# Hybrid two-layer network on one core: the scan's first convolution tap and the retention decays' clip written by ScalarE

## The reference, cut to what matters

```python
# scan: causal depthwise convolution of 4 taps over tokens, 256 channels
xp = jnp.pad(x_proj, ((0, 0), (D_CONV - 1, 0), (0, 0)))
x_conv = conv_b + sum((xp[:, k:k + l, :] * conv_w[:, k] for k in range(D_CONV)))
x_conv = _silu(x_conv)

# retention: per head and per one of 2 mixtures a decay, then a recurrence over tokens
beta = jnp.clip(jax.nn.sigmoid((x @ Wbeta.T + bbeta).reshape(b, t, NH, M)), BMIN, BMAX)   # 0.85, 0.9995
K = K * bt[..., None] + pk[:, :, None, :]
S = S * bt[..., None, None] + pk[:, :, None, :, None] * vt[:, :, None, None, :]
```

## Time and profile before

| | |
|---|---|
| median of 3 runs | 2204.74 us (2204.45 to 2205.43) |
| the profiled execution's own time | 2204.35 us |
| its span | 2202.6 us |
| busy: TensorE, VectorE, ScalarE, GpSimd | 1956.4, 1684.0, 1038.3, 491.6 us |
| mean granted TensorE clock | 0.948 of full |
| scan, first to last instruction | 0 to 206 us |
| retention | 771 to 1050 us |
| steady scan tile, from one first multiply-add of half 0 to the next (104.64 to 126.29) | 21.65 us |
| VectorE's wait for the copy L454 in the scan's tiles 1 and 3 | 1.58, 0.57 us |

### The profile page before, as it was taken

One profiled execution on the slowest core, in us unless ns is written; L12 is line 12 of the kernel. 1 busy time (PEld: TensorE's weight loads), 2 busy tenths in 40 slices (PEclk: granted clock), 3 DMA queues, 4 the chain that ended last, 5 costly groups with the idle time before them and its releaser, 6 DMA issues. The chain is left out here.

```text
span 2202.6 us, 35939 instructions
## 1 busy us (share of the span) xinstructions
PE 1956.4 (89%) x12434; PEld 1468.8 (67%) x12434; DVE 1684.0 (76%) x5253; ACT 1038.3 (47%) x1617; POOL 491.6 (22%) x556
## 2 busy tenths in 40 slices
PE   5786799998999966673899979999999999989999
PEld 3554699987899823332799955556556556559998
DVE  6997788876888879998788877766766666627887
ACT  3442244433444434442444445665655665554443
POOL 1110100012000022320200024543544544330000
PEclk8998999999999987876899989999999999989999
DMA  3000100000000010000000000000000000000000
GB/s 100 6 5 4 56 1 1 1 1 1 1 1 1 1 40 1 0 1 0 1 1 1 1 1 1 1 1 1 1 1 1 1 1 1 1 1 11 11 8 14
DMA packets 17639, 15.75 MB, mean 7 GB/s; under 512 B 4210, under 2 KB 16178, under 8 KB 16947
## 3 DMA queue, kind: packets, MB, share of 16 engines
q1 hardware_dynamic: 15152, 12.66, 1.8%
q10 hardware_dynamic: 2306, 0.78, 0.2%
HBM read 10.55 MB, written 2.88 MB: 6 GB/s over the span
## 5 line engine op out<-in xcount | busy, mean ns | idle before, releaser
L2284 DVE TENSOR_REDUCE soft_mx<-psum 128x1 f32<-128x512 f32 (+3 forms) x608 | 380.7, 659 | 196.8 <-PE psum L2153 109.3
L2199 ACT ACTIVATE soft_prob<-psum 128x1024 f32<-128x1024 f32 (+3 forms) x384 | 305.1, 813 | 205.9 <-PE psum L2079 204.8
L163 POOL TENSOR_TENSOR norm_rstd<-norm_mv,s_const_minus_half 128x4 f32<-128x4 f32 x64 | 65.2, 1019 | 916.5 <-DVE norm_mv L158 909.6
L2149 PE MATMUL psum<-soft_own,soft_stack 128*128 128x512 f32 (+3 forms) x768 | 250.3, 376 | 15.7 <-DVE soft_mx L2284 13.4
L2079 PE MATMUL psum<-soft_stack,soft_own 128*128 128x512 f32 (+3 forms) x768 | 228.4, 380 | 2.9 <-POOL soft_stack L2056 2.2
L2079 PEld LDWEIGHTS psum<-soft_stack,soft_own 128*128 128x128 f32 x768 | 121.3, 189 | 133.4 <-issue 74.5
L2149 PEld LDWEIGHTS psum<-soft_own,soft_stack 128*128 128x128 f32 x768 | 139.2, 192 | 74.3 <-DVE soft_mx L2284 59.7
L1075 DVE SCALAR_TENSOR_TENSOR x<-psum,ffn1b_cw,x 128x128 f32<-128x128 f32 x512 | 144.2, 344 | 31.3 <-PE psum L949 22.6
L2096 PE MATMUL psum<-soft_prob,soft_v_pad 128*32 128x512 f32 (+3 forms) x1536 | 163.6, 498 | 3.5 <-ACT soft_prob L2199 2.1
L1075 DVE SCALAR_TENSOR_TENSOR x<-psum,ffn0b_cw,x 128x128 f32<-128x128 f32 x512 | 144.2, 344 | 27.1 <-PE psum L949 18.4
L1075 DVE SCALAR_TENSOR_TENSOR x<-psum,ffn0a_cw,x 128x128 f32<-128x128 f32 x512 | 144.2, 344 | 27.1 <-PE psum L949 18.4
(11 more groups left out here) (377 smaller groups left out, 4055.4 us busy)
## 6 DMA issues: line engine op xcount, KB each, us to landing
s_ffn_w<-in_ffn_w SPq DMA_DIRECT2D x4, 1024.0 KB, 7.6
out_x<-x SPq DMA_DIRECT2D x8, 256.0 KB, 2.3
x<-in_x SPq DMA_DIRECT2D x4, 384.0 KB, 7.4
mamba_coef_dram<-mamba_out_coef SPq DMA_DIRECT2D x8, 96.0 KB, 1.6
s_ret_w<-in_ret_w SPq DMA_DIRECT2D x1, 640.0 KB, 3.6
x<-in_x SPq DMA_DIRECT2D x4, 128.0 KB, 3.6
s_ret_cos<-in_ret_cos SPq DMA_DIRECT2D x1, 512.0 KB, 6.8
s_ret_sin<-in_ret_sin SPq DMA_DIRECT2D x1, 512.0 KB, 6.9
```

Source lines behind the costliest of these rows:

```text
L163: self.nc.gpsimd.tensor_tensor(self.rstd[:, :], self.mv[:, :, 1], self.const["minus_half"][:, 0:GT], ALU.pow).then_inc(self.rstd_ready, 1)
L2149: ins = pe.matmul(per_head[:, n, :], stack[:, u % HT, i * P:(i + 1) * P], own[:, u % 3, g, half * BLK:half * BLK + width], start=(n == 0), ...
L2199: nc.scalar.activation(prob[:, done % PROBS, :, low(n):BLK], e_ps[:, n % 2, :, low(n):BLK], ACT.Exp, scale=float(HD) ** -0.5).then_inc(exp ...
L2284: nc.vector.tensor_reduce(mx[:, i, half, heads.start:heads.stop], bank[:, 0:width * len(heads)].rearrange("p (g k) -> p g k", k=width), AX ...
```

## The change

In the scan, ScalarE writes `w0 * xp + b` for both halves into `cv`, behind its two copies and before the tanh of the gates; VectorE's convolution begins with the second tap. In retention, ScalarE writes `relu(0.5 tanh + 0.5 - 0.85)` in place of `0.5 tanh + 0.5`, and behind the exponentials two more instructions, so that `beta` becomes `0.9995 - relu(0.1495 - relu(...))`, the same clipped value. VectorE's clip goes; three memsets make the biases.

```diff
@@ scan, ScalarE, project(a)
+                if a:
+                    act.wait_ge(xc2_ready, a)
+                for i in range(HALVES):
+                    act.wait_ge(ring_used, RING * a + i + 1)
+                    nc.scalar.activation(cv[:, i, :, :], xp[:, i, :, 0:P], ACT.Identity, scale=w["conv_w"][:, i, 0:1],
+                                         bias=w["conv_b"][:, i:i + 1]).then_inc(tap_done, 1)
@@ scan, VectorE, convolve(a, i)
-                link = Chain(dve, conv_link, CONV_STEPS * a + (CONV - 1) * i).link
-                dve.wait_ge(ring_used, RING * a + i + 1)
-                link(nc.vector.tensor_scalar(cv[:, i, :, :], xp[:, i, :, 0:P], w["conv_w"][:, i, 0:1],
-                                             w["conv_b"][:, i:i + 1], ALU.mult, ALU.add))
+                link = Chain(dve, conv_link, CONV_STEPS * a + (CONV - 2) * i).link
+                dve.wait_ge(tap_done, HALVES * a + i + 1)
@@ retention, ScalarE
-                nc.scalar.activation(beta[:, a % 2, :, :], th[:, :, :], ACT.Identity, bias=w["half"][:, :], scale=0.5)\
+                nc.scalar.activation(beta[:, a % 2, :, :], th[:, :, :], ACT.Relu, bias=clip[:, 0:1], scale=0.5)\
                     .then_inc(beta_ready, 1)
+            def clip_decays(a):
+                now = beta[:, a % 2, :, :]
+                act.wait_ge(beta_ready, a + 1)
+                nc.scalar.activation(now, now, ACT.Relu, bias=clip[:, 1:2], scale=-1.0).then_inc(narrowed, 1)
+                act.wait_ge(narrowed, a + 1)
+                nc.scalar.activation(now, now, ACT.Identity, bias=clip[:, 2:3], scale=-1.0).then_inc(clipped, 1)
...
                     exponentials(i + 1)
+                    clip_decays(i + 1)
@@ retention, VectorE
+            for i, bias in enumerate((0.5 - BETA_MIN, BETA_MAX - BETA_MIN, BETA_MAX)):
+                nc.vector.memset(clip[:, i:i + 1], bias).then_inc(clip_ready, 1)
@@ features(a)
-                dve.wait_ge(beta_ready, a + 1)
-                nc.vector.tensor_scalar(beta[:, p, :, :], beta[:, p, :, :], BETA_MIN, BETA_MAX, ALU.max, ALU.min)\
-                    .then_inc(clipped, 1)
```

More of the change, by code:

```diff
@@ L288, in mamba_scan @@
         g_ready, gt_ready, u_ready = sem("g_ready"), sem("gt_ready"), sem("u_ready")
+        tap_done = sem("tap_done")
         h_ready, hm_ready, y_ready, y_copied = sem("h_ready"), sem("hm_ready"), sem("y_ready"), sem("y_copied")
@@ L520, in _ @@
             dve.wait_ge(*all_of(*x_first))
-            STEPS, BOUND_STEPS, PREP_STEPS, CONV_STEPS = 5, 2, 13, HALVES * (CONV - 1)
+            STEPS, BOUND_STEPS, PREP_STEPS, CONV_STEPS = 5, 2, 13, HALVES * (CONV - 2)
             def tile_of(a):
@@ L1379, in retention_stage @@
         eps = sb("eps", [P, 1])
+        clip = sb("clip", [P, 3])
         shift = sb("shift", [P, GT])
@@ L1405, in retention_stage @@
         ring_ready, ring_used, tanh_done = sem("ring_ready"), sem("ring_used"), sem("tanh_done")
-        beta_ready, clipped = sem("beta_ready"), sem("clipped")
+        beta_ready, narrowed, clipped, clip_ready = sem("beta_ready"), sem("narrowed"), sem("clipped"), sem("clip_ready")
         mix_ps_ready, mix_tanh_done, mix_ready = sem("mix_ps_ready"), sem("mix_tanh_done"), sem("mix_ready")
@@ L1577, in _ @@
             act.wait_ge(weights_ready, 3)
+            act.wait_ge(clip_ready, 3)
             def scale(q):
@@ L1654, in _ @@
             exponentials(0)
+            clip_decays(0)
             copy_x(1)
```

## The result

The changed kernel takes 2217.48 us (median of five, 2214.8 to 2218.11), the kernel before 2204.77 us beside it on the same chip. The ratio is 1.0046 (95% interval 1.0035 to 1.0056), or +10 us (7.7 to 12.3); its middle is a little under the difference of the medians. The forecast was 2215.5 us, range 2206.5 to 2219. The profiled execution has a span of 2215.7 us, 13.1 us over that of before.

A forecast was written before the change was run, and what follows sets the result against it. The prediction took VectorE, gapless in steady scan tiles and retention's middle blocks, as the bound. The profiled 2204.35 us plus 10.6 for the scan and 0.5 for retention gave 2215.45, forecast 2215.5 us, range 2206.5 to 2219.

The forecast's parts named there:

- The tap, 0.80 us: Scan: one half's first convolution multiply on ScalarE takes 0.80 us, against 0.58 us on VectorE.
- Warm tile, first multiply-add 1.0 us later, wait 1.5: Scan, TensorE at full clock: VectorE waits 1.5 us for half 0's tap, half 1 saves 0.58; net +0.4 us.
- Cold tile, +1.3 each, in tiles 0, 1 and 3: Scan, projection at half clock: second copy comes late, first multiply-add 1.9 us later, net +1.3 us a tile.
- The wait of TensorE, 2.1 to 3.1 us, and a fall in five of tiles 1 to 7: Scan: TensorE's idle time before its 128x512 product grows to 3.1 us; its clock then falls to 1.2 GHz in five tiles.
- Price of a fall, 1.8 us with the slack gone: Scan: slower state products add 1.64 us, former slack 0.83 us; a warm tile with a fall costs +1.8 us in all.
- Scan +10.6: Scan's sum: 12.0 us of tap waits and clock falls, less 0.8 and 0.6 us already paid before.
- Retention +0.5: Retention: clips' savings are taken back as GpSimd's pair of 128x512 additions collides with VectorE's first recurrences; net +0.5 us.
- Cover on ScalarE, 3.35 us: Retention: ScalarE's two added instructions, 2.3 us a block, fit before a copy that waits at least 3.35 us.
- B: Rival, scan: the clock falls only where it did before; scan +6.5 us, 2211.5 us in all; chance 0.22.
- C: Rival, retention: GpSimd avoids the recurrences, 4.0 us gained; 2211 us (chance 0.12), or 2207 without added clock falls (0.13).
- D: Rival: the tap is ready when VectorE comes, all savings count; -13.3 us, 2191 us; chance 0.05.
- E: Rival: ScalarE's instruction tables are loaded anew for the tap or the relus; little chance, no size given.

The follow-up runs named there:

- e3: Changed kernel, with two 128x512 products that nobody reads given to TensorE where it waits for VectorE in the scan; ratio to the kernel before 1.0020.
- e1: Kernel before with only the scan's part of the change, retention as before; ratio to the kernel before 1.0041.
- e6: Kernel before with only half 1's first tap moved to ScalarE, retention as before; ratio to the kernel before 0.9993.
- e7: Changed kernel with each tap on ScalarE right behind its own half's copy, not behind both copies; ratio to the kernel before 1.0006.
- e11: Kernel before with half 1's tap alone on ScalarE, plus changed retention with GpSimd's second addition an iteration later; ratio to the kernel before 0.9972.
- e2: Kernel before with only retention's part of the change, scan as before; ratio to the kernel before 0.9999.
- e8: Scan as before, retention as changed, with GpSimd's second 128x512 addition one iteration later, ahead of the rotations; ratio to the kernel before 0.9988.
- e4: Changed kernel with VectorE's three copies out of PSUM ahead of half 0's convolution; ratio to the kernel before 1.0010.
- e5: Kernel before, taps and clips still on VectorE, with its three copies out of PSUM ahead of half 0's convolution; ratio to the kernel before 1.0020.
- e10: Half 1's tap alone on ScalarE, VectorE's three PSUM copies ahead of both convolutions, changed retention with its second addition moved; ratio to the kernel before 0.9978.
- e9: Changed kernel with VectorE's PSUM copies first, each tap behind its own copy, and retention's second addition moved; ratio to the kernel before 0.9979.

## Why the prediction came out right

**The tap, 0.80 us.** Right: 0.812 at the median.

**Warm tile, first multiply-add 1.0 us later, wait 1.5.** Right: the wait is 1.56 in five tiles. Half 1 saved its 0.58. Measured net, from e3's period: 22.0 - 21.65 = +0.4.

**Cold tile, +1.3 each, in tiles 0, 1 and 3.** The size was right for two: the first multiply-adds of tiles 0 and 1 come 1.16 and 2.42 us later than before (18.37 and 41.56 against 17.21 and 39.14), with waits of 3.38 and 4.00 us. The third was at another place and larger. Tile 3 was warm, tile 6 cold, with a wait of 3.07, 1.5 us more than in a warm tile, where the prediction had 0.9 more; which tile's projection runs cold changes from run to run.

**The wait of TensorE, 2.1 to 3.1 us, and a fall in five of tiles 1 to 7.** Right: 3.06 us in five of the seven, and five falls, 1 to 4 and 7. The rule behind the count was too plain, and the trace of before already spoke against it. I argued that a stretch of 3.1 us is followed by a fall because the five of 2.7 us and more that I had read all were. But in that trace, in retention, two stretches ahead of the same products go the other way (eight of 512 columns, 3.67 us long where the granted clock is 1.00):

```profile
771.45 3.67 PE L1494 MATMUL psum<-norm_xt,s_ret_w 128*128 128x512 f32 x8 [2.87 <-DVE norm_pause L135]
...
871.93 5.53 PE L1494 MATMUL psum<-norm_xt,s_ret_w 128*128 128x512 f32 x8 [2.30 <-DVE ret_kv L1715]
```

The clock held after 2.87 us and had fallen after 2.30. And the stretches of 2.11 us that I counted as one fall in six are five in that trace. In the changed kernel tile 5 held after 3.06 us, tile 6 after 2.73, and tile 1 fell after 2.14; e1 held twice after 3.06. Over the scans with idle times of 2.64 to 3.06 us ahead of the product (6 tiles of the changed kernel, 7 of e1), 8 of 13 fell. At 2.2 us and under it was one in seven before, in e6 and in e7, two in e11, and none in e2 and e8: 5 of 42. Five falls was a likely count that I gave as a sure one; that it came out at five and not at e1's four is luck.

**Price of a fall, 1.8 us with the slack gone.** Right, and measured twice: the period is 23.43 to 23.45 us with a fall (1.8 over before's), and against e3, where the clock holds, tiles 1 to 4 are 1.38 to 1.43 us longer where 1.4 was forecast (1.8 less the 0.4 that stays). Only tile 7's fall costs more, 2.1 us. The rest of the 7.75 us is scatter: 0.35 ahead of the first multiply-add, and 0.34 the other way around the cold projection, which e3 has in tile 7 and the changed kernel in tile 6.

**Scan +10.6.** Measured +12.3 in the profiled execution, +10.4 in e1. This term was 1.7 us short of the one and right by the other. Its own sum holds 5.0 us of waits (1.3 + 1.3 + 6 x 0.4), 7.0 us of clock (5 x 1.4) and takes off 1.4, so 3.6 and 7.0. e3 measures 4.6 and 7.75. Both were short. The waits were short because the sum leaves out the third cold tile that the prediction itself names ("three in all"): all of tiles 2 to 7 go in at the warm 0.4, and tile 6 waited 1.5 us more, while tiles 0 and 1 stayed some 0.5 under. The clock was short because of tile 7, where I had assumed a warm tile like the others: L645 waits 2.05 us for the products and L566 1.66 for the step inputs, of which 1.46 were there before; in tile 4 the two are 0.67 and 0.63. VectorE has no norm of a later tile to do there, so less covers a long L407.

**Retention +0.5.** Right within what the runs resolve: +0.3 in the profiled pair, and seven blocks at a mean of 212.2 us in five kernels with the changed retention and the pair in place (changed, e2, e3, e4, e7) against 211.6 in four with the old one (before, e1, e5, e6). Its working holds part by part: the power 1.92 us (1.91 foreseen), blocks 31.95 us apart against 31.6 (+0.35, foreseen +0.3). That it was the collision with the pair is shown by e8. By the exclusive lock that the prediction takes from the Trainium skill, "SBUF — State Buffer", § SBUF: two separate sides, the power has to wait for VectorE's instruction on two SBUF tensors. The trace agrees: the power, four elements a partition, lasts 1.92 us beside an instruction of 1.22, and 1.01 at its shortest. One piece doesn't hold: the first block's -0.4 us. That block is 22.13 us long instead of 22.50, as foreseen, but e1 and e6 have 22.12 with the clip in place, so the clip's going isn't shown to be the cause.

**Cover on ScalarE, 3.35 us.** It held: the copy of the sums that had waited 3.35 us still waits 1.38 in the changed kernel, and no instruction of VectorE waits for a clip.

**The rivals.** B (the clock falls no more than before) is near to what e3 made by hand; without the falls the scan would have lost 4.6 us. C (no collision) is near to e8: 4.6 us were to be had, but not by this change alone. D, the tap ready in time, is nearest in e6, for half 1 alone. E is out: the changed kernel has the same 17 table loads, 16 of them at the logarithm and the exponential of retention's sums.

**What a single time is worth here.** Between the scan and retention all kernels run the same instructions. From mamba_output's first product of y and the gate to VectorE's first instruction of retention it took 560.4 us before and 560.5 in the changed kernel, but 560.0 in e5, 561.3 to 561.7 in e2, e8, e10 and e11, and 562.3 to 563.0 in e1, e3, e4, e6, e7 and e9. From retention's eighth features to the end, again nearly the same instructions, it took 1206.8 and 1206.7 us, and 1202.9 (e6) to 1207.5 (e4) in the others. What makes these 3 and 4.6 us isn't known. They show how far a kernel's time and its mark can part: e6's profiled execution took 2198.68 us, the lowest of its eleven, with a median of 2201.87, and e7's 2202.79, with 2206.23.

## What to carry to other kernels

Before moving an instruction to an engine with time to spare, look at what stands ahead of it in that engine's order when its reader comes, and put it behind its own input, not behind its neighbour's; here that decided between 10 to 12 us of loss and about none. Move first the one of several that is due last (e6's mark says so, its time alone doesn't). And follow the wait one engine on: most of the loss (7.75 of 12.3 us) was on TensorE, whose idle time grew by 1 us, and in retention the gain went to an engine that the diff doesn't touch.

## What the runs showed of the hardware

- After idle stretches of the same 3.06 us TensorE's granted clock fell to the 1.2 GHz level in some tiles and held in others, within one execution (e1: 6.23, then 4.59 us for the same products). Short waits were followed by falls too. In e10 waits of 1.00, 1.40 and 1.03 us within ten microseconds were the longest of a tile, and the clock fell ahead of all six of tiles 2 to 7; in e4 and e9, with the same waits, ahead of two of six each. Behind waits of about 1.02 and 1.03 us the projection of before, e2 and e8 ran at the lower level in 6 tiles of 18.
- Two products that nobody reads, in a wait of 3.06 us, went with state products of 4.59 us in all seven tiles and took 7.75 us off the scan's mark (e3). One projection still ran at the lower level (3.68 us, tile 7). The two products cost nothing that could be seen, since TensorE was waiting.
- The power of retention in the changed kernel, by source line (min/median/max ns):

```profile
L1462 POOL TENSOR_TENSOR ret_z_rstd<-ret_z_mv,s_const_minus_half x8: 1008/1922/1925, 849.5 to 1058.5; 128x4 f32<-128x4 f32 x8
```

- This GpSimd instruction on four elements a partition lasted 1.92 us where VectorE had started an instruction on two SBUF tensors 0.17 us earlier; its shortest took 1.01. A 128x512 addition lasted 2.25 us instead of 1.27 when a recurrence had just begun, and the next recurrence waited for it in turn: the two engines took turns by instruction.
